# Raw scores and maxima of a unit begin two steps ahead, two pairs in every step

## What is computed

```python
q = Wq @ layernorm(x) + bq;  k = Wk @ ctx + bk;  v = Wv @ ctx + bv      # (256, 512) a batch
dot = einsum('bhdt,bhds->bhts', q, k) / 4
dot = mask * dot - (1 - mask) * 1e6
x = x + einsum('bhts,bhds->bhdt', softmax(dot) * mask, v)
h = layernorm(x)                                                       # rows of 512
probs = softmax(h @ gate_w.T);  topw, sel = top_k(probs, 2);  topw /= sum(topw)
x = x + sum over the two experts of topw * (silu(g) * u) @ w2,  g, u = split(h @ w1)
```

## Time and profile before

| | us |
|---|---|
| median of 3 runs | 1061.33 (1051.53 to 1066.79) |
| the profiled execution | 1049.48, its span 1047.7 |
| PE busy | 847.7 (81%) |
| DVE busy | 546.1 (52%) |
| POOL busy | 368.3 (35%) |
| ACT busy | 312.8 (30%) |
| the attention part, to the first expert tile | about 716 |
| the 36 expert tiles, from there to the end | about 332 |

### The profile page before, as it was taken

How to read it: one execution, slowest core, us unless ns; L and a number is a source line. 1 busy time by engine, 2 the same in 40 slices (tenths; PEclk the granted TensorE clock), 3 DMA queues, 4 the chain that set the end, 5 groups by cost and what they waited for, 6 DMA issues and landing times. The chain is left out here.

```text
span 1047.7 us, 13045 instructions
## 1 busy us (share of the span) xinstructions
PE 847.7 (81%) x3720; PEld 371.2 (35%) x3721; DVE 546.1 (52%) x1133; ACT 312.8 (30%) x615; POOL 368.3 (35%) x380
## 2 busy tenths in 40 slices
PE   2077978988988788789888888515999999999995
PEld 0022323322332232233233222213555555555552
DVE  3084767767777578667767875241232323322222
ACT  0003554544455345355445556400000000000000
POOL 6244225535634635734733622230111111111111
PEclk9567998998999899999999999856999999999998
DMA  6422553654654645654453442232353544544332
GB/s 170 118 65 65 151 161 117 177 149 129 195 153 123 183 112 161 186 141 106 143 151 101 123 131 78 89 114 66 61 137 66 143 104 99 143 107 96 60 60 40
DMA packets 73257, 125.08 MB, mean 119 GB/s; under 512 B 15712, under 2 KB 29552, under 8 KB 73208
## 3 DMA queue, kind: packets, MB, share of 16 engines
q1 hardware_dynamic: 39432, 69.65, 24.7%
q10 hardware_dynamic: 26032, 36.98, 11.7%
q0 software_dynamic: 7744, 17.86, 8.9%
HBM read 77.34 MB, written 46.72 MB: 118 GB/s over the span
## 5 line engine op out<-in xcount | busy, mean ns | idle before, releaser
L697 DVE TENSOR_REDUCE mx<-tile 128x2 f32<-128x1024 f32 x256 | 306.6, 1216 | 125.6 <-PE tile L975 121.7
L585 ACT ACTIVATE pr<-sc 128x512 f32<-128x512 f32 x512 | 267.7, 603 | 271.7 <-PE sc L962 271.2
L975 PE MATMUL tile<-ks,qs 97*128 97x512 bf16 x512 | 164.2, 414 | 38.3 <-DMA ks<-mrow_d 28.1
L962 PE MATMUL sc<-qs,ks 100*128 100x512 bf16 x512 | 164.2, 402 | 36.8 <-DMA qs<-mxt 27.7
L1265 POOL DMA_INDIRECT out_dram<-y,ids x36 | 56.1, 1558 | 283.9 <-DVE ids L1190 279.8
L991 PE MATMUL pvb<-pr,vp 128*32 128x512 f32 x1024 | 142.0, 628 | 0.0
L485 POOL TENSOR_TENSOR att<-num,rb 128x512 f32<-128x512 f32 x16 | 20.2, 1265 | 270.0 <-DMA rb<-recip_d 270.0
L1315 PE MATMUL dp<-wring,at 128*128 (+1 forms) x216 | 102.2, 609 | 13.4 <-DVE at L1200 13.4
L1245 ACT ACTIVATE sg<-gp 128x352 f32<-128x352 f32 x36 | 16.7, 463 | 292.0 <-PE up L1294 292.0
L975 PEld LDWEIGHTS tile<-ks,qs 97*128 97x128 bf16 x512 | 41.8, 102 | 171.6 <-DVE mx L697 71.5
L962 PEld LDWEIGHTS sc<-qs,ks 100*128 100x128 bf16 x512 | 49.2, 103 | 141.5 <-ACT pr L585 64.7
(11 more groups left out here) (117 smaller groups left out, 731.0 us busy)
## 6 DMA issues: line engine op xcount, KB each, us to landing
split_d<-parts SPq DMA_DIRECT2D x96, 128.0 KB
wring<-w_dram SPq DMA_DIRECT2D x32, 352.0 KB, 5.1
xl<-routed_d ACTq DMA_DIRECT2D x38, 257.0 KB, 2.7
pv_d<-ov ACTq DMA_DIRECT2D x32, 256.0 KB, 3.6
qs<-split_d SPq DMA_DIRECT2D x32, 192.0 KB
ks<-split_d SPq DMA_DIRECT2D x32, 192.0 KB
xin<-x_dram SPq DMA_DIRECT2D x16, 256.0 KB, 9.6
cin<-ctxt_dram SPq DMA_DIRECT2D x8, 512.0 KB, 4.9
```

What stands on the lines that cost most here:

```text
L585: nc.scalar.activation(pr[s % 2][:, j, :], sc[(32 * u + 4 * s + j) % NSC][:, :], ACT.Exp, scale=SCALE).then_inc(exped.sem, 1)
L697: dve.tensor_reduce(mx[:, 2 * j:2 * j + 2], t[:, :, :], X, ALU.max, negate=True).then_inc(drained.sem, 1)
L962: nc.tensor.matmul(sc[(32 * u + 4 * s + j) % NSC][:, :], ks[half(u)][0:ALL_ROWS, h, c * P:c * P + P], qs[half(u)][0:ALL_ROWS, h, :], start ...
L975: last = nc.tensor.matmul(t[:, i, :], qs[half(w)][0:RAW_ROWS, h, c * P:c * P + P], ks[half(w)][0:RAW_ROWS, h, :], start=True, stop=True)
```

## The change

The number of raw pairs in a step becomes two everywhere. The pairs 0 to 3 of a unit move to the seventh and eighth step of the loop's unit before, so a loop unit `u` now holds pairs 4 to 15 of unit `u+1` in its first six steps and pairs 0 to 3 of unit `u+2` in its last two (`pairs_of`, `unit_of`); `mx` gets a second buffer. The split and the transpose of the maxima come in the seventh step, the last product of a unit in the first step of the next, v in the second step, q, now of unit `u+3`, in the fourth, tokens and logits in the fifth and sixth, and k, of unit `u+3` too, at the end of the eighth. The stores of q's and k's parts are two functions of their own on SyncE (`keep_split`), k's ahead of the first stack and q's behind it. The maxima go out in one DMA. GpSimd takes k's parts first and the inverse deviation of tokens ahead of the scatter. The counts of tokens an expert are no longer kept by VectorE: GpSimd sums the choices in `before`, a matmul with `ones` adds them to the ranks, and one more matmul after the last unit gives the totals. The gap of the two best logits is taken inside the exponential, and the two selections are one operation. Of VectorE's part of the diff the removed lines are left out; its former order stands in the functions above.

```diff
@@ -42,7 +42,8 @@
 ICHUNKS = [(0, 128), (128, 128), (256, 96)]
 FIRST, LAST = -5, UNITS + 2
 CHUNKS = 6
-SHARE = [2, 3, 2, 3, 3, 2, 1, 0]
+NPAIR = 16
+LEAD = 4
 NSLOT = 2
 NSC = 3
 
@@ -85,22 +86,38 @@
         return self.step * len(self.no)
 
 
+def pairs_of(n, s):
+
+
+    first = LEAD + 2 * s
+    if first < NPAIR:
+        return [first, first + 1] if has(n + 1) else []
+    return [first - NPAIR, first - NPAIR + 1] if has(n + 2) else []
+
+
+def unit_of(n, m):
+
+    return n + 1 if m >= LEAD else n + 2
+
+
 def tile_events(n):
-    ev, m = [], 0
-    for s, k in enumerate(SHARE):
-        if has(n + 1):
-            ev += [("max", m + j) for j in range(k)]
-            m += k
-        if s == 0 and has(n + 2):
+    ev = []
+    for s in range(8):
+        max_ = [("max", m) for m in pairs_of(n, s)]
+        if s == 7:
+            ev += max_[:1] + ["ranks"] * has(n - 2) + max_[1:] + ["k"] * has(n + 3)
+            continue
+        ev += max_
+        if s == 1 and has(n + 1):
+            ev.append("v")
+        if s == 3 and has(n + 3):
             ev.append("q")
-        if s == 1 and has(n + 2):
-            ev.append("k")
-        if s == 3 and has(n - 2):
+        if s == 4 and has(n - 2):
             ev.append("xT")
-        if s == 4 and has(n - 2):
+        if s == 5 and has(n - 2):
             ev.append("logits")
-        if s == 7:
-            ev += ["maxT"] * has(n + 1) + ["ranks"] * has(n - 2) + ["v"] * has(n + 1)
+        if s == 6 and has(n + 1):
+            ev.append("maxT")
     return ev
 
...
@@ -344,10 +363,19 @@
                                  mrow_d[side:side + 1, batch(w):batch(w) + 1, :].broadcast_to([1, 4, T])
                                  ).then_inc(stacked[g].sem, 16)
 
+            def keep_split(u, side):
+
+                w = u + 3 - side
+
+                if (due := stacked[1].at(w - 3, "g")) is not None:
+                    sp.wait_ge(stacked[1].sem, due)
+                sp.wait_ge(split[side].sem, split[side].at(u, 3))
+                for i in range(3):
+                    sp.dma_start(split_d[half(w), side, i].rearrange("d h t -> h d t"),
+                                 parts[:, side, i, :]).then_inc(split_kept[side].sem, 16)
+
             def unit(u):
                 if has(u + 1):
-
-                    sp.wait_ge(split_kept.sem, split_kept.at(u - 1, "split"))
                     stack(u + 1, 1)
                 if half(u) and has(u + 3):
                     load_ctx(u)
@@ -357,28 +385,20 @@
                     if 0 <= n < WRING * CHUNKS:
                         load_expert(sp, n // CHUNKS, n % CHUNKS)
                 if has(u + 2):
-                    w = u + 2
-
-                    for g in range(2):
-                        if (due := stacked[g].at(u - 2 + g, "g")) is not None:
-                            sp.wait_ge(stacked[g].sem, due)
-                    for side in range(2):
-                        sp.wait_ge(split.sem, split.at(u, (side, 3)))
-                        for i in range(3):
-                            sp.dma_start(split_d[half(w), side, i].rearrange("d h t -> h d t"),
-                                         parts[:, side, i, :]).then_inc(split_kept.sem, 16)
-                    sp.wait_ge(split_kept.sem, split_kept.at(u, "split"))
-                    stack(w, 0)
+                    keep_split(u, 1)
+                    sp.wait_ge(split_kept[0].sem, split_kept[0].at(u - 1, "k"))
+                    sp.wait_ge(split_kept[1].sem, split_kept[1].at(u, "k"))
+                    stack(u + 2, 0)
+                if has(u + 3):
+                    keep_split(u, 0)
                 if has(u + 1):
                     w = u + 1
                     sp.wait_ge(drained.sem, drained.at(u, "maxT"))
 
                     if (due := scored.at(u - 1, (7, 3))) is not None:
                         sp.wait_ge(scored.sem, due)
-                    for i in range(3):
-                        sp.dma_start(qs[half(w)][MAX_ROW + i:MAX_ROW + i + 1, :, :]
-                                     .rearrange("o h (c t) -> o (h c) t", t=P),
-                                     mxt[32 * i:32 * i + 32, :]).then_inc(maxrows.sem, 16)
+                    sp.dma_start(qs[half(w)][MAX_ROW:MAX_ROW + 3, :, :].rearrange("o h (c t) -> o (h c) t", t=P),
+                                 mxt[:, :]).then_inc(maxrows.sem, 16)
 
...
 
             def scatter(u):
                 v = u - 3
+                pool.wait_ge(const_made, MADE)
+                pool.wait_ge(ready.sem, ready.at(u - 1, "ranks"))
+                pool.tensor_tensor(before[:, :], before[:, :], selb[:, :], ALU.add).then_inc(summed.sem, 1)
                 pool.tensor_copy(xa[:, half(v), :, T + 1:T + 2],
                                  io[:, 80 + v:81 + v].rearrange("p (a o) -> p a o", a=1)
...
             for u in range(FIRST, LAST + 1):
-                if has(u):
+                if has(u + 2):
+                    part(u, 1)
+                if has(u - 2):
+                    token_rstd(u)
+                if has(u + 1):
                     values_out(u)
                 if has(u - 3):
                     scatter(u)
-                if has(u + 4):
+                if has(u + 5):
                     batch_rstd(u)
-                if has(u - 2):
-                    token_rstd(u)
-                if has(u + 2):
+                if has(u + 3):
                     part(u, 0)
-                    part(u, 1)
...
                             nc.scalar.activation(pr[s % 2][:, j, :], sc[(32 * u + 4 * s + j) % NSC][:, :],
                                                  ACT.Exp, scale=SCALE).then_inc(exped.sem, 1)
-                        if (s, j) == (4, 0) and has(u - 2):
+                        if (s, j) == (5, 0) and has(u - 2):
                             transposed_out(u)
-                    if s == 0 and has(u - 2):
-                        store_x1(u)
+                    if s == 0 and has(u - 1):
+                        product_out(u - 1, 1)
                     if s == 1 and has(u - 1):
                         load_product(u)
+                    if s == 2 and has(u - 2):
+                        store_x1(u)
                     if s == 4 and has(u):
                         product_out(u, 0)
                     if s == 4 and has(u - 1):
                         store_recip(u)
-                    if s == 6 and has(u - 1):
+                    if s == 5 and has(u - 1):
                         load_recip(u)
-                if has(u - 2):
-                    gate_weight(u)
-                if has(u):
-                    product_out(u, 1)
+                    if s == 7 and has(u - 2):
+                        gate_weight(u)
...
             def unit(u):
+                maximum(u, 4)
+                maximum(u, 5)
+                maximum(u, 6)
+                token_stats(u, 0)
+                maximum(u, 7)
+                token_stats(u, 1)
+                values_out(u)
+                maximum(u, 8)
+                token_normalize(u, 0)
+                maximum(u, 9)
+                token_normalize(u, 1)
+                maximum(u, 10)
+                batch_stats(u, 0)
+                reciprocals(u, 0)
+                maximum(u, 11)
+                batch_stats(u, 1)
+                reciprocals(u, 1)
+                projection_out(u, 0)
+                maximum(u, 12)
+                maximum(u, 13)
+                maximum(u, 14)
+                normalize(u)
+                maximum(u, 15)
+                choose(u, 0)
+                split_maxima(u, 0)
+                choose(u, 1)
+                split_maxima(u, 1)
+                choose(u, 2)
+                split_maxima(u, 2)
+                choose(u, 3)
+                split_maxima(u, 3)
                 maximum(u, 0)
+                choose(u, 4)
                 maximum(u, 1)
+                choose(u, 5)
+                maxima_out(u)
                 maximum(u, 2)
+                rows_of(u, 0)
                 maximum(u, 3)
+                rows_of(u, 1)
                 projection_out(u, 1)
...
             dve.wait_ge(const_made, MADE)
             for u in range(FIRST + 1, LAST + 1):
                 unit(u)
-            dve.wait_ge(drained.sem, drained.total())
+            dve.wait_ge(counted, 1)
+            dve.tensor_copy(counts[:, :], tiles[0][:, 0, 0:E]).then_inc(counted, 1)
+            dve.wait_ge(counted, 2)
             plan_tiles()
 
...
@@ -1046,8 +1069,12 @@
                     return
                 pe.wait_ge(choice.sem, choice.at(u, "selb"))
                 t = slot(u, "ranks")
-                nc.tensor.matmul(t[:, 0, 0:E], upper[:, :], selb[:, :], start=True, stop=True)
-                nc.tensor.matmul(t[:, 0, E:2 * E], ones[:, :], selb[:, :], start=True, stop=True
+
+                if (due := summed.at(u, "s")) is not None:
+                    pe.wait_ge(summed.sem, due)
+                nc.tensor.matmul(t[:, 0, 0:E], ones[0:1, :], first[:, :], start=True, stop=False)
```

(51 more changed lines are left out.)

215 lines of the change are left out of this document (89 added, 126 removed).

## The result

The changed kernel takes 1087.32 us, the median of 4 runs (1079.34 to 1095.08), beside 1059.34 for the kernel before (4 runs, 1051.53 to 1066.79). The ratio is 1.0264, with a 95% interval of 1.0156 to 1.0373. I had forecast 1030 us and a range up to 1083.

The account below looks back on a forecast made before the run. It took a chain of transfers to bound the kernel: 37.4 us a unit falling to 35.5. Gains of 28 in units, -3 at the start, +1 for unit 14 and +5.5 at the end made 31.5 us: 1030 us, range 985 to 1083.

Parts of the forecast that it names:

- The transfers after: Attention units after the change: chain of transfers from one raw pair 0 to the next, 35.5 us a unit, the bound.
- Pair 0 to the maxima's DMA: Chain's first term: pairs 0 and 1, transpose of the maxima, copy and issue of one DMA, 4.5 us.
- Second stack: Chain term: a unit's second layout of q and k by DMAs, right behind the maxima, 13.9 us.
- Its landing to the first stack's issue: Chain terms: loads behind the second stack 2 us, k's split issue and landing 4.1, less 1 for overlap.
- First stack: Chain's last stack term, after k's split is stored: 12 us, between bounds 11.7 and 14.1.
- TensorE waits at pairs 0 and 8: TensorE stands for a late stack at raw pairs 0 and 8, 2 to 4 us each, in most units.
- Engines' pace 31.5: Attention units: pace of TensorE and VectorE after the change, 31.5 us a unit, bounds 29.7 and 34.6.
- Start: Start of attention: first exact score at about 87 instead of 84.35, 3 us lost, bounds 0 and 8.
- Tail: End of attention: GpSimd computes the inverse deviation ahead of the scatter, 5.5 us gained, bounds 0 and 7.
- The slower one: Rival, 13%: two stacks in one chain round, at 15.8 us each; 41.2 us a unit, 1115 us.
- The one on the maxima: Rival, 10%: maxima in one DMA land late, 7.8 us against a cover of 4.6; 38.7 a unit, 1077 us.
- clause on the 48-row part of a stack: Within the 10% rival on late maxima: this part, its source repeating three times, goes over few DMA engines; no size given.

Follow-up runs that it names:

- a_lp2: Changed kernel with ScalarE's load of the product (den, num, xr) after step 2 instead of step 1; 0.9987 of the kernel before.
- a_rc6: Changed kernel with the reciprocals' load after ScalarE's step 6 instead of step 5; 1.0015 of the kernel before.
- a_both: Changed kernel with both the product's and the reciprocals' load a step later; 0.9796 of the kernel before, 1030.25 us.
- c_spread: Changed kernel with both loads later, maxima transposed ahead of raw pairs 0 and 1, q's stack rows in six 16-row DMAs; 0.9121 of the kernel before, 958.05 us.
- a_spboth: Changed kernel with q's stack rows in six 16-row DMAs and both ScalarE loads a step later; 0.9218 of the kernel before, 966.20 us.
- c_maxt: Changed kernel with both loads a step later and the maxima transposed ahead of raw pairs 0 and 1; 0.9597 of the kernel before, 1011.28 us.
- a_spread: Changed kernel with q's stack rows in six DMAs of 16 rows instead of three of 48, 32 and 16; 0.9455 of the kernel before, 989.57 us.
- b_spread: Kernel before with q's stack rows in six DMAs of 16 rows instead of three of 48, 32 and 16; 0.9569 of the kernel before, 1005.18 us.

## Why the prediction was wrong

**What failed is the chain of "The transfers after", 35.5 us a unit.** One round of it in the changed kernel, from raw pair 0 to the next:

```profile
405.63 0.59 PE L998 MATMUL tile<-ks,qs 97*128 97x512 bf16 x2 [0.17 <-DVE lg L763]
413.07 0.78 SPq L400 DMA_DIRECT2D qs<-mxt  x1
413.89 1.86 SPq L360 DMA_DIRECT2D qs<-split_d  x3
425.73 0.60 PE L998 MATMUL tile<-ks,qs 97*128 97x512 bf16 x2 [0.94 <-DMA ks<-mrow_d]
433.43 1.06 PE L985 MATMUL sc<-qs,ks 100*128 100x512 bf16 x2
434.58 1.89 SPq L360 DMA_DIRECT2D qs<-split_d  x3
446.67 0.60 PE L998 MATMUL tile<-ks,qs 97*128 97x512 bf16 x2 [0.83 <-DMA ks<-mrow_d]
```

- *Pair 0 to the maxima's DMA*: 4.5 forecast, 7.4 measured. ScalarE's wait for the reciprocals and the slow clock lie in it (0.79 granted from 405 to 413 us).
- *Second stack*: 13.9 forecast; 12.7 with the maxima's issue ahead of it.
- *Its landing to the first stack's issue*: 2 + 4.1 - 1 forecast, 8.9 measured. Not k's split held it (its stores were issued at 423.07 and had landed at 430.64) but the exact scores of the fourth step (433.43), which the stack may not overtake, and these were late by ScalarE's wait for the product's store. The scores are what ends last in ten of the 14 units that wait for some; in the other four it is k's stores, by 0.2 to 0.7 us.
- *First stack*: 12 forecast, 12.1 measured.

The sum is 41.0 against 35.5: the two terms that hold a ScalarE wait are 6.7 over, the second stack 1.2 under. So the step that failed is one that the prediction never took: it counted VectorE's, TensorE's and SyncE's moved work and passed over `product_out`, `load_product` and `load_recip`, whose waits it thus put at nothing; they cost some 2.8 and 2.5 points of time (`a_lp2`, `a_rc6`). For the product the rows were there: the store issued at 386.20 in the kernel before landed after 7.7 us,

```profile
pv_d<-ov ACTq DMA_DIRECT2D x1, 256.0 KB, 7.7
```

and its load followed 7.8 us later, with nothing to spare. By the semaphore events the load left within 0.1 us of the landing in six units of 16 before and in all 16 now. For the reciprocals no row showed it: their store landed in a median of 2.4 us before and in 5.6 after, since it now leaves beside a stack in 13 units and not in 3.

With the two waits taken out (`a_both`) the kernel takes 1030.25 us at 36.1 a unit: the chain of 35.5 was then about right in its sum. Its terms were less so. The 13.9 and 14.1 that it called the common values of a stack are high: by the semaphore events the first stacks of the kernel before take 10.3 to 14.9 us, median 11.6, and both kinds in the changed kernel 12. And k's stores, 4.1 in the sum, take 4.3 to 13.3, median 7.0. The one error made up for the other. That 1030.25 is also the forecast time is partly luck.

**Point by point.** *The wait for the maxima goes*: right; also with one DMA for three rows. *TensorE waits at pairs 0 and 8*: the places were right, the size under the 2 to 4 each (32.6 us in 21 waits). *First stack about 14 us into a unit*: wrong, 18.2 (434.58 less 416.41). *Engines' pace 31.5*: close, as far as other orders can tell: 31.8 in `c_spread`, 32.4 in `a_spboth`. *Start*: 3 forecast, 8.4 measured, just past its bound of 8: four maxima of the next unit and k's projection now stand ahead of the first scores, and they wait for that unit's first stack (raw pair 0 at 83.32 after 2.52 of wait). The early transpose does not help there (`c_maxt` 93.21). Quick stacks do (`a_spread`), but they help the kernel before at least as much (`b_spread`); first line `a_spread`, second `b_spread`:

```profile
85.78 1.06 PE L986 MATMUL sc<-qs,ks 100*128 100x512 bf16 x2
75.97 1.03 PE L963 MATMUL sc<-qs,ks 100*128 100x512 bf16 x2 [0.25 <-DMA qs<-mxt]
```

With quick stacks the change still loses 9.8 us at the start: this loss is the order's own.

*Tail*: the inverse does follow at once, and from the last statistics to the counts it takes 8.0 us instead of 11.5:

```profile
734.46 0.18 DVE L694 BATCH_NORM_AGGREGATE l<-l 128x2 f32<-128x6 f32 x1
734.73 0.23 POOL L480 TENSOR_SCALAR l<-l 128x1 f32<-128x1 f32 x1 [1.03 <-DVE l L694]
742.25 0.17 DVE L956 COPY counts<-tile 128x8 f32<-128x8 f32 x1
```

3.5 of the 5.5 forecast; but the last unit up to its last store (717.12) takes 27.5 instead of 23.3, at a granted clock of 0.88 instead of 1.00, and takes it back.

**The rivals.** The slower one had the right sign and the wrong mechanism: the stacks did not grow to 15.8 us. The one on the maxima cited the rule that turned out to matter most, and applied it to 24 KB. There the trace agrees on the shape (the one DMA steps its semaphore 4 times, where each of the three before did so 16 times), but it landed in 2.9 to 3.2 us, inside the cover of 4.6. The rival's clause on the 48-row part of a stack was left without a price. Added to the changed kernel alone, the cut is worth 98 of the 129 us from 1087 to 958; added last (`c_maxt` to `c_spread`), 53. Slow stacks bounded the kernel before as well (`b_spread`), where I took 13.9 us for a stack's own time and never asked why 768 KB should need it.

Left open: how the gain of the cut divides between the stacks themselves and the stores beside them; no run took the one without the other. With both loads already moved the cut still gives 5.8 points (`a_both` to `a_spboth`) of the 8.1 that it gives without, so most of it does not go by these two waits.

## What to carry to other kernels

When a step is moved, walk every in-order queue that it issues on, and measure the distance from each store to the load that waits for it against that store's own landing in the trace, not the median; then ask what work covers that wait now and whether the same change removes the cover, or puts the store beside a large transfer. When a transfer takes long for its bytes at a moderate mean DMA share, look at its shape before its schedule: one whose source repeats a few large pieces can be cut into pieces whose first dimension is 16 rows. Only after that is an order of work worth tuning: the same change cost 2.6 points with the slow stacks and nothing that can be seen with the quick ones.

## What the chip showed that I had not expected

Cutting three DMAs with a repeated source into six made other DMAs faster: on ScalarE's queue the stores of 256 KB from 5.7 to 2.1 us (first halves) and from 6.5 to 4.1 (second halves) and those of 16 KB from 5.6 to 1.9, and the loads of x, issued on the same queue as the stacks, from 8.1 to 3.5. And TensorE's clock followed: 0.84 granted between 300 and 550 us in the changed kernel, 0.98 and 1.00 in `a_spread` and `c_spread`, once most of the short stalls were gone.
